# A decoder layer on one core: the three order tables of a planned kernel, written anew

## What is computed

```
x = layernorm(x + linear_attention(x))     # 16 heads of 64; q' = exp(q wq_feat), k' = exp(k wk_feat), 32 features
x = layernorm(x + cross_attention(x, ctx)) # 16 heads of 8; softmax over 64 context tokens
x = layernorm(x + ffn(x))                  # 128 -> 512, gelu, layer norm, 512 -> 128, ternary weights
```

## Time and profile before

| | |
|---|---|
| Median of 3 runs | 620.47 us (619.85 to 620.98) |
| Profiled execution | 619.85 us, span 617.4 us, granted TensorE clock 0.987 in the mean |
| Busy | PE 591.3, DVE 479.2, ACT 464.6, POOL 487.3 us |
| Instructions | 31077, of them 13344 matmuls |

### The profile page before, as it was taken

How to read it: one execution, slowest core, us unless ns; L and a number is a source line. 1 busy time by engine, 2 the same in 40 slices (tenths; PEclk the granted TensorE clock), 3 DMA queues, 4 the chain that set the end, 5 groups by cost and what they waited for, 6 DMA issues and landing times.

```text
span 617.4 us, 31077 instructions
## 1 busy us (share of the span) xinstructions
PE 591.3 (96%) x13344; PEld 433.7 (70%) x13344; DVE 479.2 (78%) x1235; ACT 464.6 (75%) x875; POOL 487.3 (79%) x653
## 2 busy tenths in 40 slices
PE   9999999999999999999999999999999999997684
PEld 6686767777677867767686867767686857665554
DVE  2555677887888887888878887888878887988676
ACT  3636566978878797878879787878879787959563
POOL 5065144798989998898989999999988989998845
PEclk9999999999999999999999999999999999999699
DMA  8113222353544536363554646363644636254501
GB/s 337 72 37 114 64 80 72 79 142 73 132 87 123 115 107 130 76 161 73 134 94 131 116 100 136 70 168 73 134 88 135 118 79 123 63 124 78 98 18 53
DMA packets 116154, 64.89 MB, mean 105 GB/s; under 512 B 94321, under 2 KB 100850, under 8 KB 115890
## 3 DMA queue, kind: packets, MB, share of 16 engines
q1 hardware_dynamic: 116018, 62.91, 42.9%
HBM read 17.27 MB, written 4.19 MB: 35 GB/s over the span
## 4 chain that ended last, share of the span: by engine, by line
PE 71%; POOL 14%; ACT 5%; issue 4%; DMA 4%; DVE 2%; SPq 1%; POOLq 0%; ACTq 0%; DVEq 0%
PE bank L337 15%; PE bank L327 8%; PE bank L357 8%; PE bank L449 4%; POOL gall L1185 3%; ACT PT L665 3%; POOL gs L1190 2%; PE bank L318 2%; PE bank L435 2%; PE bank L414 2%; PE bank L276 2%; PE bank L492 2%; PE bank L278 2%; PE bank L277 2%; DMA pack<-Mrow 2%
## 5 line engine op out<-in xcount | busy, mean ns | idle before, releaser
L337 PE MATMUL bank<-Mh,GT 128*32 128x128 f32 x4096 | 128.6, 274 | 0.0
L337 PEld LDWEIGHTS bank<-Mh,GT 128*32 128x32 f32 x4096 | 107.1, 110 | 18.5 <-issue 14.3
L918 DVE TENSOR_REDUCE mx<-bank 128x8 f32<-128x512 f32 x128 | 79.0, 682 | 16.3 <-PE bank L414 16.2
L665 ACT ACTIVATE PT<-bank 128x512 f32<-128x512 f32 x128 | 64.4, 625 | 16.8 <-PE bank L435 16.8
L550 ACT ACTIVATE GT<-bank 128x512 f32<-128x512 f32 x95 | 51.8, 596 | 29.4 <-PE bank L327 26.9
L1185 POOL TENSOR_TENSOR gall<-gall,lnr 128x512 f32<-128x512 f32 x56 | 73.2, 1310 | 0.5 <-DVE st L853 0.5
L1190 POOL TENSOR_TENSOR gs<-gall,gs 128x512 f16<-128x512 f32 x56 | 64.9, 1161 | 9.5 <-ACT gs L702 9.4
L550 ACT ACTIVATE Cb<-bank 128x512 f32<-128x512 f32 x66 | 39.0, 594 | 43.7 <-PE bank L357 29.4
L327 PE MATMUL bank<-kp,xs 64*128 64x512 f32 x256 | 70.6, 627 | 0.0
L1132 POOL TENSOR_TENSOR rstd<-ve,mhalf 128x4 f32<-128x4 f32 x60 | 61.3, 1022 | 5.0
L357 PE MATMUL bank<-Cb,qT 128*64 128x128 f32 x1024 | 59.4, 274 | 0.0
(11 more groups left out here) (203 smaller groups left out, 1524.9 us busy)
## 6 DMA issues: line engine op xcount, KB each, us to landing
pack<-Qh SPq DMA_DIRECT2D x64, 128.0 KB, 2.6
xT<-in_xT SPq DMA_DIRECT2D x16, 256.0 KB, 3.0
xs<-in_x_nat SPq DMA_DIRECT2D x16, 256.0 KB, 3.0
cxT<-in_cxT SPq DMA_DIRECT2D x16, 256.0 KB, 3.0
Kp<-Kh SPq DMA_DIRECT2D x32, 128.0 KB, 2.1
pack<-Ql SPq DMA_DIRECT2D x32, 128.0 KB, 2.9
out_y<-yo SPq DMA_DIRECT2D x15, 256.0 KB, 2.4
Kp<-Kl SPq DMA_DIRECT2D x16, 128.0 KB, 2.1
```

Source lines behind the costliest of these rows:

```text
L337: m = e.matmul(bk[32 * j:32 * j + 32, tile(g_)], GT[b % 4][:, tile(hh, 32)], Mh[:, tile(hh)], start=True, stop=True)
L665: e.activation(PT[tp][:, tile(j, 512)], bank[uses["prob", s, i][0]][:, :], ACT.Exp, scale=SM).then_inc(emptied("prob", s, i)[0], 1)
L918: e.tensor_reduce(to, bank[uses["score", s, i][0]][:, :].rearrange("p (g b k) -> p g b k", g=2, b=4), AX.X, ALU.max).then_inc(emptied("sco ...
```

## The change

The three strings are replaced; everything else stays. The set of TensorE steps is the same. What moves, apart from the order:

- PERIOD, TensorE: down0@3 and down1@3 stand ahead of bc in place of behind prob1; g4 and g5 open the round, directly behind prob1 of the round before; c1, ks, pv0 follow, c2 and c3 come behind the four up steps; vproj stands ahead of rows, and all of k0 to k3 ahead of score0.
- PERIOD, POOL: x1s@1, csplit, ab2@3, gs0 to gs2, cs0, stat, gl0, gl1 in a row; split@-2 stands at the end of the round, behind st1, where split@-1 stood at the beginning of the next one behind x1s and ab2.
- PERIOD, SP: the load of the context behind rows; the DMA of rows ahead of the transposes of gl2 and gl3.
- PERIOD, copies: c2 and c4 go to ScalarE, c5 to VectorE, ap3@5 to VectorE.
- HEAD: wq ahead of wb, all of k0 to k3 ahead of mh0, small2 loaded ahead of Wff, sbar ahead of o, bias3 behind it, GpSimd's xb ahead of qz; x1s of group 0 is left to PERIOD.
- TAIL: another order throughout; the second half of ap1 of group 15 is on VectorE, flip's copy on ScalarE, vproj@1 stands behind proj1@2, up0@2 ahead of prob0@1, and ap3@3 on VectorE.

```diff
--- before.py
+++ after.py
@@ -33,25 +33,25 @@
 
 
 HEAD = """
-wk wb wq k0 k1 k2 WkT g0 zeros g1 g2+ mh0 split small1 mh1 g3+ k3 q0 c0+ c1+ WqT split@1 loadx Wvp ks c2 Wff c3 xw loadx@1 kst g4+ g5 g6+ small2 g7+
-q1 k0@1 q2 q3 gam g0+@1 bv g1+@1 k1@1 c4+ c5+ dT nbeta qz loadc k2@1 bias3 bias2 bc c6 c7+ biasA o g2+@1 xb csplit loadx@2 st1 g3@1 kproj k3@1 ap1+
-loadc@1 x1s csplit@1 sbar vproj c0@1 kpack loadc@2
+WkT wk wq wb k0 k1 small1 k2 k3 q0 mh0 g0 mh1 g1 g2 xw g3 g4 g5+ WqT q1 zeros loadx c0+ c1+ c2+ ks Wvp small2 c3+ Wff g6+ g7+ kst q2 q3 loadx@1 loadc
+split gam bv csplit c4+ c5+ split@1 c6+ nbeta loadc@1 k0@1 bias2 c7 dT g0+@1 g1@1 k1@1 biasA xb bc qz sbar o g2+@1 g3+@1 st1 k2@1 k3@1 kproj ap1+
+vproj bias3 loadx@2 c0@1 kpack split@2
 """
 PERIOD = """
-split@-1 c1 c2 ks pv0@2 g4 g5 up0@3 down2@4 up1@3 gs0@3 down3@4 up2@3 up3@3 q0 stat@3 c3 cs0@2 kst ab1@1 pv1@2 oturn0@2 q1 gs1@3 q2 qproj@1 q3 gh0@3
-qpack@1 c4 ap3+@5 oturn1@2 c5+ dT g6+ g7+ kproj k0@-1 cs1@2 kpack gl0@3 vproj proj0@2 k1@-1 gl1@3 k2@-1 score0@1 gs2@3 gh1@3 loadx@-2 c6+ c7+ score1@1
-xb g0+@-1 g1+@-1 g2+@-1 gs3@3 gh2@3 g3+@-1 proj1@2 gl2@3 k3@-1 st2@2 rows@1 gl3@3 gh3@3 csplit@-1 bc c0+@-1 ap2+@2 o prob0@1 st1 prob1@1 down0@3 st3@4
-x1s loadc@-2 ab2@2 down1@3 ap1+
+ap3@5 g4 g5 x1s@1 csplit down2@4 q0 c1 ab2@3 gs0@3 ks pv0@2 up0@3 gs1@3 gs2@3 up1@3 kst cs0@2 qpack@1 down3@4 up2@3 stat@3 gl0@3 up3@3 c2+ gl1@3 c3
+pv1@2 q1 q2 oturn0@2 qproj@1 q3 gh0@3 c4+ c5 dT gh1@3 oturn1@2 cs1@2 g6+ g7+ k0@-1 xb proj0@2 k1@-1 kproj k2@-1 k3@-1 score0@1 loadx@-2 c6+ ab1@1 c7+
+score1@1 gs3@3 g0+@-1 g1+@-1 g2+@-1 g3+@-1 gh2@3 kpack proj1@2 st2@2 vproj rows@1 loadc@-1 gh3@3 down0@3 gl2@3 gl3@3 ap2+@2 down1@3 bc c0+@-1 st3@4 o
+st1 prob0@1 prob1@1 ap1+ split@-2
 """
 TAIL = """
-down2@5 c1@1 ks@1 pv0@3 pv1@3 cs0@3 up0@4 cs1@3 gs0@4 tw@1 up1@4 up2@4 oturn0@3 qpack@2 oturn1@3 kpack@1 g4+@1 ap3+@6 c2+@1 down3@5 stat@4 gs1@4 up3@4
-kproj@1 qproj@2 c3@1 proj0@3 kst@1 q0@1 c4+@1 proj1@3 gh0@4 q1@1 g5+@1 g6@1 gs2@4 gl0@4 q2@1 g7+@1 q3@1 st2@3 score0@2 c5+@1 dT@1 gl1@4 score1@2 gh1@4
-gh2@4 c6+@1 c7+@1 xb@1 gs3@4 bc@1 rows@2 gl2@4 o@1 ap2+@3 gl3@4 gh3@4 st1h0@1 prob0@2 down0@4 st1h1@1 st3@5 prob1@2 ap1h0+@1 ap1h1+@1 down1@4 down2@4
-ab2@3 pv0@2 ab1@2 oturn0@2 pv1@2 up0@3 gs0@3 down3@4 up1@3 flip@1 qpack@1 gs1@3 stat@3 up2@3 up3@3 gl0@3 qproj@1 oturn1@2 vproj@1 proj0@2 ap3+@5
-proj1@2 gl1@3 st2@2 gh0@3 gh1@3 gs2@3 score0@1 score1@1 ap2+@2 gh2@3 down0@3 rows@1 gs3@3 gh3@3 flip3@2 gl2@3 down1@3 gl3@3 ab2@2 prob0@1 ab1@1
-prob1@1 st3@4 down2@3 pv0@1 up0@2 oturn0@1 down3@3 pv1@1 proj0@1 up1@2 ap3+@4 oturn1@1 up2@2 st2h0@1 up3@2 ap2h0+@1 proj1@1 st2h1@1 turn0+@2 turn1+@2
-st3@3 ap2h1+@1 stat@2 flip3h0@1 turn2+@2 turn3@2 flip3h1@1 down0@2 up0@1 ab2h0@1 down1@2 up1@1 ab2h1@1 up2@1 down2@2 up3@1 ap3+@3 down3@2 turn0+@1
-st3@2 turn1+@1 stath0@1 stath1@1 down0@1 down1@1 turn2+@1 turn3+@1 ap3+@2 down2@1 st3h0@1 down3@1 st3h1@1 ap3h0@1 ap3h1@1
+ap3@6 g4@1 down2@5 csplit@1 x1s@2 q0@1 qpack@2 xb@1 gs0@4 cs0@3 up0@4 pv0@3 down3@5 oturn0@3 c1+@1 gs1@4 tw@1 ks@1 ab2@4 up1@4 up2@4 up3@4 stat@4
+gh0@4 kproj@1 kpack@1 gl0@4 pv1@3 c2@1 qproj@2 q1@1 g5+@1 g6+@1 proj0@3 q2@1 q3@1 kst@1 c3@1 cs1@3 oturn1@3 gs2@4 c4+@1 c5+@1 c6@1 gh1@4 ab1@2
+score0@2 gl1@4 dT@1 gl2@4 score1@2 gs3@4 proj1@3 gh2@4 g7+@1 c7+@1 rows@2 st2@3 gl3@4 gh3@4 bc@1 o@1 ap2+@3 st1h0@1 prob0@2 prob1@2 st1h1@1 ab2@3
+qpack@1 ap1h0+@1 st3@5 gs0@3 pv0@2 down0@4 down1@4 gs1@3 gl0@3 gl1@3 down2@4 up0@3 ap1h1@1 down3@4 flip+@1 up1@3 up2@3 oturn0@2 up3@3 stat@3 qproj@1
+gh0@3 pv1@2 oturn1@2 proj0@2 proj1@2 st2@2 gh1@3 ap3+@5 vproj@1 ap2+@2 score0@1 score1@1 gh2@3 down0@3 flip3@2 rows@1 gh3@3 gs2@3 gs3@3 up0@2 down1@3
+gl2@3 ab1@1 gl3@3 st3@4 prob0@1 ab2@2 prob1@1 turn0@2 down2@3 pv0@1 oturn0@1 down3@3 pv1@1 proj0@1 oturn1@1 st2h0@1 up1@2 ap3+@4 turn1+@2 proj1@1
+st2h1@1 st3@3 up2@2 turn2+@2 stat@2 ab2h0@1 up3@2 ap2h0+@1 ap2h1+@1 flip3h0@1 ap3@3 flip3h1@1 down0@2 turn3+@2 down1@2 down2@2 up0@1 down3@2 turn0+@1
+st3@2 stath0@1 stath1@1 up1@1 up2@1 turn1+@1 down0@1 turn2+@1 up3@1 ap3+@2 down1@1 down2@1 ab2h1@1 st3h0@1 turn3+@1 down3@1 st3h1@1 ap3h0@1 ap3h1@1
 """
 
 
```

## The result

| | before | after |
|---|---|---|
| Median | 620.49 us (619.85 to 620.98, 4 runs) | 630.56 us (626.33 to 631.52, 4 runs) |
| Ratio after/before | | 1.0146, 95% interval 1.0112 to 1.0180 |
| Profiled execution | 619.85 us, span 617.4, clock 0.987 | 631.23 us, span 629.4, clock 0.974 |

The time lies above the whole range of the forecast (613.8 to 623). I split the two profiled spans at the first matmul of each prob, numbered by its group.

A forecast was written before the change was run, and what follows sets the result against it. TensorE's full queue was taken as the bound, 34.69 us a round at best. Middle -1.6, head -0.3 and tail -0.4 gave -2.3 us: median 618.2 from 620.47, own range 616 to 620.3, 0.8 range 613.8 to 623.

The forecast's parts named there:

- Middle, own time: TensorE's steady rounds: new neighbour pairs against the removed pace of down0 and down1, +0.05 us a round, between -0.1 and +0.3.
- The seam: g4 and g5 directly behind prob: a pair at 0.53 us each finds its banks free; 0, at most 0.1 more a round.
- the pair above 1.1 us: Sign: a pair of g behind prob taking more than 1.1 us would refute the seam estimate.
- the other side: Rival, chance 0.15: down0 and down1 wait for gT in the middle, each us paid 13 times; 627 us.
- Mrow: Middle: TensorE's waits for the Mrow transfer ahead of prob go; gain 0.17 us a round, at most 0.20.
- Covers: Moved work in the rounds comes in time for TensorE, at no cost; thinnest is gl1's transpose before down1, 0.6 to 2 us.
- VectorE: Sharing with GpSimd in a round: up to 1 us lost at the KSz product, some at ap3; no cost to TensorE.
- Head: Start of the run: same steps reordered, two c steps fewer behind fp16; -0.3 us, between -1 and +1.
- Tail: Last stretch: chain of group 15 1.3 us earlier, less 0.9 for a pair of down steps; -0.4 us, between -4 and +4.
- The walk for group 15: Tail chain from ap1 to ap3 walked with earlier durations: proj1 1.2 us earlier, last down 1.3 earlier.
- the prediction's own sign: Tail: last middle prob to the end should be 1.3 us shorter than 93.4; if longer, the walk was wrong.
- Clock: Tail: granted clock is 0.50 after TensorE's first wait, so what falls beside it costs double; 1 us of matmul is 2.

The follow-up runs named there:

- a_head: The kernel before with only the new HEAD, its end fitted to the old PERIOD; 620.05 us, ratio 0.9994.
- e_hg7: a_head with gh2 of group 12 moved behind the copy c7+ of group 15 in TAIL; 619.22 us, ratio 0.9989.
- e_mixg7: d_mix with gh2 of group 12 moved behind the copy c7+ of group 15 in TAIL; 619.67 us, ratio 0.9993.
- d_mix: The kernel before with the new HEAD and the new TAIL's order from prob of group 14 to proj1 of group 15; 620.59 us, ratio 0.9995.
- b_seam: The kernel after with g4 and g5 behind down2 and q0 in PERIOD, not directly behind prob1; 627.88 us, ratio to before 1.0119.
- b_gseam: The kernel before with g4 and g5 of the next group directly behind prob1, ahead of down0; 639.75 us, ratio 1.0306.
- a_tail: The kernel before with only the new TAIL, without the steps the old PERIOD has done; 623.93 us, ratio 1.0052.
- d_end: a_tail with the old ending back behind proj1 of group 15; 624.83 us, ratio to before 1.0053.
- c_g7: The kernel after with gh2 of group 12 behind the copies g7+ and c7+ of group 15 in TAIL; 627.37 us, ratio to before 1.0107.
- a_period: The kernel before with only the new PERIOD, HEAD and TAIL of before fitted to it; 625.63 us, ratio 1.0077.

## Why the prediction was wrong, step by step

- *Middle, own time* (+0.05 a round for new pairs): right. Without the pair behind prob, the steps of a round add up to 34.66 us, 0.03 below's best. down1 before bc costs 0.09, rows before down0 nothing.
- *The seam* ("g5 finds its bank just free. I take 0; it costs at most 0.1 more a round"): **the step that failed first.** I read the pair's 1.06 as two steps of 0.53 in sequence, so g5 would be asked for 0.53 us after g4. The two run at once, so g5 wants its bank together with g4 and gets it half a microsecond late. It cost 0.47 a round, 6 us over 13 rounds, and was above even the upper bound of +0.3 a round. Of the prediction's signs, the pair above 1.1 us was the right one; rounds above 35 were to mean the other side, and here they came without any wait for gT.
- *Mrow* (-0.17 a round): right as to the mechanism; the wait is gone in all rounds. But it was not the new PERIOD's to win: with the old one, a_head's rounds are at 34.69 to 34.72 in eight of eleven cases, and all eleven of e_hg7 and of e_mixg7 are at 34.68 to 34.73. All three have the new HEAD, yet d_mix has it too and still has rounds of 35.19 and 35.10; what decides it is open.
- *Covers*: right. TensorE never waited for gT or x1T in the middle, so the rival of the other side (down0 and down1 waiting) did not come. b_seam shows how near it is for down2.
- *VectorE*: ap3 took 0.28 us a piece (1.12 for four at 355.53) without a stall. The product for KSz did lose time, as the prediction allowed: 0.65 us in nearly every round where it was 0.28, with no cost on TensorE. What I did not see is its copy of g5 waiting 1.6 to 1.9 us a round for c1, free of cost here and dear in b_gseam.
- *Head* (-0.3): +0.3 to +0.5 by the order, and 1.03 by the moment of the clock's rise, which differs between executions and so is luck; a_head as a whole is 0.9994.
- *Tail* (-0.4, bounds -4 and +4): **the second failure,** +7.4 us in the profile for equal work, +3.2 by a_tail. The walk for group 15 was fair up to proj1 (0.9 us earlier counted from prob of group 14, forecast 1.2). Its last down was to end 1.3 earlier and ended 0.1 earlier in a_tail, since the up steps of group 15 now stand one by one between turns, and TensorE waits for their gelus (the row of L499 below; 0.7 in d_end). But the large loss is in a stretch that I had not walked. Between prob of groups 13 and 14 I counted TensorE's work alone, and it lost 6.2 us, 7.2 for equal work, to the other engines' queues and the clock. The wait of gh2 is one cause that the traces show; how the rest divides is open. By the prediction's own sign the walk was wrong: from prob of group 13 to the end it takes 99.8 us, not 1.3 less than 93.4.
- *Clock*: the earlier trace rows told me that what falls beside the low clock costs double. I used it for the old low stretch only, and left out that a new wait makes a new one: the clock fell during the 2.8 us before c7, and in c_g7, where TensorE waits 0.8 us there, it did not.

The row of PE's waits in after, from 567 us on, for the ending:

```profile
PE bank L499 <- ACT gall L689: 1.8, 3, 0.8
```

The sum was forecast at -2.3 and is +12.0 in the profiles, 14.3 apart: 4.6 in the middle (the seam's 6.1, less 1.5 that the rest gained beyond the forecast), 1.9 in the head (1.0 of it from before the first k), 7.8 in the tail.

## What to carry to other kernels

Two matmuls in different row halves are one step of the array: both banks must be free at the moment of the first. Read the pair's start-to-start time with a partner missing before giving it a price. When a schedule is rewritten, walk every in-order queue from the last steady round to the end, for what stands behind each wait for a DMA. A full busy share with no waits is not proof of a full engine: compare start to start, group by group.

## What was not expected of the hardware

- A bank wait of the second of two side-by-side matmuls is in no view of waits: 0.47 us a round show only as busy time of L327 (76.5 us against 70.6 with a mean of 626 and 627 ns).
- The spacing of the same 25 matmuls halved at 4.0 us from the start in one execution and at 6.1 in another, and not before the last of them in a third (a_period). With the old HEAD in the first and the third, the first matmul of k came at 9.20 and 10.45 us.
- The same program took near 631 us in 15 of 37 executions and near 627 in 10, with mean clocks of 0.974 and of 0.985 or above; the other 12 lie between. The kernel before stays within 617.9 to 623.1 in the 92 runs made beside the experiments.
